# Attention: VectorE's merge of an old unit queued ahead of the newest unit's maximum, and the normalising product of finished rows on GpSimd

## The reference

```
xn = layernorm(x)
q_c = rms_norm(xn @ wq_down.T);  kv_c = rms_norm(xn @ wkv_down.T)
q = [q_c @ wq_up.T | rope(q_c @ wq_rope.T)]          # 16 heads, 128 + 64
k = [kv_c @ wkv_up.T (first 128) | rope(xn @ wk_rope.T)];  v = the other 128
s = softmax(causal(q k^T / sqrt(192))) v, all heads, @ wo.T
g = silu(((silu((xn @ gate_w.T) * gate_s) * ((xn @ up_w.T) * up_s)) @ down_w.T) * down_s)
out = x + s * g
```

## Time and profile before

| | |
|---|---|
| median of the runs shown | 4944.75 us (3 runs: 4944.75, 4978.76, 4425.7) |
| the profiled execution's own time | 4418.68 us |
| span of its slowest core (core 4) | 4417.1 us |
| spans of the eight cores | 4358.2 to 4417.1 us |
| TensorE busy, in the span | 3703.2 us (84%) |
| VectorE busy | 1585.0 us (36%) |
| ScalarE busy | 1189.8 us (27%) |
| GpSimd busy | 382.1 us (9%) |

### The profile page before, as it was taken

The page is one execution under the profiler, slowest core; times in us unless marked ns, Lnnn a source line. Parts: engine busy times, 40 slices in busy tenths (PEclk is TensorE's granted clock), DMA queues, the critical chain, the costliest instruction groups (busy, mean ns, idle before and its releaser), DMA issues.

```text
span 4417.1 us, 57223 instructions; the slowest of 8 cores (4358.2 to 4417.1 us)
## 1 busy us (share of the span) xinstructions
PE 3703.2 (84%) x21727; PEld 1878.3 (43%) x22128; DVE 1585.0 (36%) x3298; ACT 1189.8 (27%) x1591; POOL 382.1 (9%) x487
## 2 busy tenths in 40 slices
PE   1777877777777777777769999999799999999898
PEld 0333334444444444444434444444344444444343
DVE  2445334777677777667821111100001111110000
ACT  1222205555565555555610000000000000000000
POOL 0212230000000000000001111100010000000001
PEclk9888889999999999999989999999899999999999
DMA  8554254676666666676688887865664444435564
GB/s 180 143 141 126 79 138 77 111 114 116 118 114 112 110 108 114 113 116 111 115 153 127 126 128 121 136 204 181 205 194 129 77 77 77 77 68 175 183 194 143
DMA packets 783194, 566.59 MB, mean 128 GB/s; under 512 B 689744, under 2 KB 698192, under 8 KB 773072
## 3 DMA queue, kind: packets, MB, share of 16 engines
q1 hardware_dynamic: 711840, 318.04, 33.5%
q0 software_dynamic: 42288, 171.46, 22.2%
q10 hardware_dynamic: 28800, 73.41, 5.3%
HBM read 499.34 MB, written 73.40 MB: 130 GB/s over the span
## 4 chain that ended last, share of the span: by engine, by line
PE 67%; DVE 16%; DMA 12%; issue 3%; ACT 1%; SPq 0%; POOL 0%; ACTq 0%; DVEq 0%; POOLq 0%
PE bk L1076 25%; PE bk L1096 12%; DVE nmx L897 9%; PE bk L1115 5%; PE ps_s L833 4%; PE ps_o L885 3%; PE ps_mm L427 3%; DMA dw<-d 3%; PE ps_s L838 2%; PE ps_s L867 2%; PE ps_s L845 2%; PE ps_s L864 2%; DMA uw<-upP 2%; DMA pt<-pp 2%; PE ps_kv L427 2%
## 5 line engine op out<-in xcount | busy, mean ns | idle before, releaser
L897 DVE TENSOR_REDUCE nmx<-ps_s 128x1 f32<-128x1024 f32 (+3 forms) x640 | 678.4, 1060 | 416.3 <-PE ps_s L867 254.1
L940 ACT ACTIVATE pp<-ps_s,bia,scq 128x1024 bf16<-128x1024 f32 (+3 forms) x640 | 686.2, 1074 | 525.3 <-DVE bia L901 266.9
L1076 PE MATMUL bk<-xc,gw 128*128 128x512 bf16 x2759 | 639.7, 382 | 53.5 <-DMA uw<-upP 50.6
L1096 PE MATMUL bk<-dw,hdn 128*128 128x512 bf16 x2760 | 615.1, 381 | 52.3 <-DMA dw<-d 48.1
L885 PE MATMUL ps_o<-vv,pt 128*128 128x129 bf16 x4352 | 361.3, 222 | 333.5 <-DVE ost L928 180.6
L1076 PE MATMUL bk<-xc,uw 128*128 128x512 bf16 x2759 | 632.4, 379 | 3.0
L1132 DVE SCALAR_TENSOR_TENSOR hdn<-bk,us_s,sg 128x512 bf16<-128x512 f32 x176 | 131.8, 750 | 1141.7 <-PE bk L1076 1061.9
L885 PEld LDWEIGHTS ps_o<-vv,pt 128*128 128x128 bf16 x4352 | 275.7, 98 | 505.9 <-issue 478.9
L1076 PEld LDWEIGHTS bk<-xc,gw 128*128 128x128 bf16 x2816 | 276.7, 98 | 390.0 <-issue 64.1
L1096 PEld LDWEIGHTS bk<-dw,hdn 128*128 128x128 bf16 x2816 | 275.3, 98 | 390.1 <-issue 66.0
L1164 ACT ACTIVATE sg<-bk,gs_s 128x512 f32<-128x512 f32 x176 | 120.7, 687 | 1110.9 <-PE bk L1076 1067.2
(11 more groups left out here) (101 smaller groups left out, 2663.6 us busy)
## 6 DMA issues: line engine op xcount, KB each, us to landing
dw<-d SPq DMA_DIRECT2D x176, 512.0 KB, 4.8
gw<-gateP POOLq DMA_DIRECT2D x88, 512.0 KB, 6.2
uw<-upP POOLq DMA_DIRECT2D x88, 512.0 KB, 8.4
xb<-xk ACTq DMA_DIRECT2D x32, 1024.0 KB, 6.3
wo_s<-wo SPq DMA_DIRECT2D x16, 2048.0 KB, 9.1
d<-downP POOLq DMA_DIRECT2D x44, 512.0 KB, 12.3
xo<-xk ACTq DMA_DIRECT2D x64, 256.0 KB, 4.4
out<-xo ACTq DMA_DIRECT2D x64, 256.0 KB, 5.7
```

The source lines that it names most:

```text
L897: kb.go(e, lambda: e.tensor_reduce(nmx[n % 8][:], r3(buf(ev_)[:], 2)[:, :, 0:w], AX.XY, ALU.max, negate=True), [("p", f"b_s_{n}")], "v")
L940: kb.go(e, lambda: e.activation(r3(pp[n % NP][:, 0:2 * w], 2), r3(buf(ev_)[:], 2)[:, :, 0:w], AF.Exp, bias=bia[n % 8][:], scale=scq[:, i:i ...
L1076: mm_ = e.matmul(bk[pr * 2 + z][:], W[u_i % 2][:, dc * 128:(dc + 1) * 128], xc[hf][:, dc * 512:(dc + 1) * 512], start=(dc == 0), stop=(dc ...
L1096: mm_ = e.matmul(bk[tt][:], hdn[:, ic * 1024 + hf * 512 + tt * 128: ic * 1024 + hf * 512 + (tt + 1) * 128], dw[q % 3][:, (ic % 4) * 512:(i ...
```

## The change

Four things are done.

1. In `steps()` the merge event of a round is put first: merge(n - 7), S(n), PV(n - 6), piece. On VectorE the merge of unit n - 7 now stands ahead of the maximum of unit n. TensorE's and ScalarE's own orders stay as they are.
2. The normalising product goes from VectorE to GpSimd, a row of the new loop in `b_gp` for each block, and reads oacc and linv from SBUF. So blocks of one unit also are copied to oacc first, and their reciprocal reads oacc. oacc and linv get four buffers; the first merge of a block waits for the product of the block four rows before.
3. The semaphore mark b_mg of a unit is now on its merge in every case; before, that of a block's last unit was on the product.
4. GpSimd's loads and stores stand between the products: the load of wup behind the second product of a head, qp behind the third, the store of the head before behind the seventh. SyncE's transpose of ost is issued one round later and waits for GpSimd's last product.

```diff
-            oacc = [sb(f"oacc{i}", [128, VS], F32) for i in range(3)]
+            oacc = [sb(f"oacc{i}", [128, VS], F32) for i in range(4)]
...
-            linv = [sb(f"linv{i}", [128, 1], F32) for i in range(2)]
+            linv = [sb(f"linv{i}", [128, 1], F32) for i in range(4)]
...
                 for n in range(NU + LAG + 1):
+                    if n >= LAG + 1:
+                        ev.append(("merge", n - LAG - 1))
                     if n < NU:
                         ev.append(("S", n))
                     if n >= LAG and n - LAG < NU:
                         ev.append(("PV", n - LAG))
-                    if n >= LAG + 1:
-                        ev.append(("merge", n - LAG - 1))
...
-                    if ot_next < NH and n >= LASTU[ot_next] + LAG + 3:
+                    if ot_next < NH and n >= LASTU[ot_next] + LAG + 4:
                         h = ot_next
-                        kb.wait(e, "v", f"b_mg_{LASTU[h]}")
+                        kb.wait(e, "g", f"b_on_{h * NB + NB - 1}")
...
                 for h in range(NH):
-                    if h + 2 < NH:
-                        kb.wait(e, "p", f"b_pc_{h}_{NPC - 1}")
-                        load_wup(e, h + 2)
-                    if 1 <= h and h + 1 < NH:
-                        kb.wait(e, "p", f"b_s_{LASTU[h - 1]}")
-                        load_qp(h + 1)
-                    if h >= 1:
-                        store_o(h - 1)
+                    for oi, i in enumerate(BORDER):
+                        row = h * NB + oi
+                        if oi == 0:
+                            kb.wait(e, f"ot{h % 2}", f"b_ot_{h - 2}")
+                        kb.go(e, lambda: e.tensor_scalar(ost[h % 2][:, i * 128:(i + 1) * 128],
+                                                         oacc[row % 4][:, 0:128], linv[row % 4][:], None,
+                                                         ALU.mult, ALU.bypass),
+                              [("g", SELF), ("v", f"b_li_{row}")], "g", f"b_on_{row}")
+                        if oi == 1 and h + 2 < NH:
+                            kb.wait(e, "p", f"b_pc_{h}_{NPC - 1}")
+                            load_wup(e, h + 2)
+                        if oi == 2 and 1 <= h and h + 1 < NH:
+                            kb.wait(e, "p", f"b_s_{LASTU[h - 1]}")
+                            load_qp(h + 1)
+                        if oi == 6 and h >= 1:
+                            store_o(h - 1)
...
-                        if s_ == 0 and ns > 1:
+                        if s_ == 0:
+                            kb.wait(e, "g", f"b_on_{row - 4}")
                             kb.go(e, lambda: e.tensor_copy(A[:, 0:129], O[:, 0:129]),
                                   [("p", f"b_pv_{n}")], "v", f"b_mg_{n}")
-                        elif s_ > 0:
+                        else:
...
                         if s_ == ns - 1:
-                            src = A if ns > 1 else O
-                            L = linv[row % 2]
-                            kb.go(e, lambda: e.reciprocal(L[:], src[:, 128:129]),
-                                  [("p", f"b_pv_{n}"), ("v", SELF)], "v")
-                            kb.go(e, lambda: e.tensor_scalar(dst, src[:, 0:128], L[:], None,
-                                                             ALU.mult, ALU.bypass),
-                                  [("v", SELF)], "v", f"b_mg_{n}")
+                            kb.go(e, lambda: e.reciprocal(linv[row % 4][:], A[:, 128:129]),
+                                  [("v", SELF)], "v", f"b_li_{row}")
```

More of the change, by code:

```diff
@@ L769, in b_sync @@
                 ot_next = 0
-                for n in range(NU + LAG + 4):
+                for n in range(NU + LAG + 5):
                     if n < NU:
@@ L910, in b_vec @@
                         h, i, s_, ns, row = UNITS[n]
-                        A = oacc[row % 3]
+                        A = oacc[row % 4]
                         O = ps_o[n % 2]
-                        dst = ost[h % 2][:, i * 128:(i + 1) * 128]
-                        if n % PER_H == 0:
-                            kb.wait(e, f"ot{h % 2}", f"b_ot_{h - 2}")
-                        if s_ == 0 and ns > 1:
+                        if s_ == 0:
+                            kb.wait(e, "g", f"b_on_{row - 4}")
                             kb.go(e, lambda: e.tensor_copy(A[:, 0:129], O[:, 0:129]),
                                   [("p", f"b_pv_{n}")], "v", f"b_mg_{n}")
-                        elif s_ > 0:
+                        else:
                             kb.go(e, lambda: e.scalar_tensor_tensor(A[:, 0:129], A[:, 0:129], fac[n % 8][:],
```

## The result

The changed kernel is **faster: the ratio to the kernel before is 0.9601, with a 95% interval of 0.956 to 0.9641**. The forecast, 4240 on the level of 4418.7, was a ratio of 0.9596. The profiled execution took 4246.79 us (before 4418.68), 171.9 us less where 177 were forecast. The medians of the runs, 4258.85 us now and 4689.09 us before, hold some executions in which the cores of one die had a lower clock, so the ratio is taken from the others: 4246.3 to 4263.4 us now, 4425.7 and 4433.4 before.

The account below looks back on a forecast made before the run. The loop of maximum, merge and PV between VectorE and TensorE was taken to bound heads with projections. Savings of 153 + 3 + 35 less 14 for DMA make 177 us off 4418.7: 4242, said as 4240, range 4160 to 4335.

Parts of the forecast that it names:

- The bound: In heads 0 to 14 VectorE and TensorE wait for each other in turn, so each projection piece is paid in full.
- part 1: Merge queued ahead of the maximum on VectorE: 10.2 us saved in each of 15 heads, 153 us, and 3 in head 15.
- q pieces: Two projection pieces a head of 24 wide matmuls, 5.2 us each: after the change 3.76 us lost each, 7.5 a head.
- short pieces: Eight projection pieces a head of eight wide matmuls, 1.73 us each: after the change 0.6 us lost each, 4.8 a head.
- the 24.2 us of before: Price of a head's pieces before the change, eight of 1.73 and two of 5.2 us, against 22.5 us seen.
- the ring of score buffers: Three buffers, so scores of round n need the exponential of n-3: the next edge, leaving a lead of 1.44 us.
- Part 2: Normalising product off VectorE: 3.2 us off, 1.0 on for copies, net 2.2 us a head, 35 us in 16 heads.
- Part 3: DMA, the load of wup in its new place among the transposes: 1 us a head added, 14 us, bounds -2 and +5.
- rival (c): The load's stall grows by 5 us a head in its new place: 4296 us, 4310 with the clock's price; chance 0.11.
- (a): GpSimd's product locks VectorE's bias out through a shared port: 26 us at most for the product's bounds; chance 0.05.
- (b): The lead doesn't open because another edge binds where the merge did; only the product's gain stays: 4384 us; chance 0.12.
- (d): Short pieces vanish wholly and q pieces mostly, so a head comes near TensorE's own time, 77 us: 4147 us; chance 0.10.

Follow-up runs that it names:

- the three products: The changed kernel with each normalising product on GpSimd issued three times, holding the same values: no ratio, two shortest executions 4254.26 and 4227.25 us.
- the best version: The changed kernel with the load of wup behind the sixth product, the ring's mark ahead of fac and q pieces halved: ratio 0.9423, 4139.8 to 4150.5 us.

## Why the prediction came out as it did

**The bound and part 1: right.** The heads were bound by the loop of maximum, merge and PV. The order alone took 9.8 us off an undisturbed head against 10.2, and 2.9 off head 15 against 3. The terms hold as well: in head 14 of that kernel VectorE idles 3.9 and 4.1 us behind the two q pieces, 8.0 where 7.5 were worked out, and 5.2 us otherwise, where 4.8 were put for the short pieces. (One price was off there: I put all eight short pieces at 1.73 us, but the four of v take 1.95 by the earlier trace rows, which makes the 24.2 us of before 25.1.) The long waits that are left stand behind q pieces, as the model had it (in the changed kernel a q piece at 1435.6 in head 8 is followed by a maximum after 4.43 us of idling; 3.76 were worked out). The next edge is the ring of score buffers, as said. What I left out there is that the ring's mark is on fac, 0.28 us behind the exponential, where I took 0.1 us for the whole hand-over. The run with the mark moved prices that at 1.25 us a head. Take it off the 13.3 us of idling in the run with the order alone and 12.0 are left, against 12.3 in the model. That subtraction is an estimate, for the mark wasn't moved in that kernel.

**Part 2: mis-sized.** The step that failed is "from one to the next maximum 0.20, so 3.2 us off", with "a copy and the wait of the reciprocal for it 1.0 us on". VectorE's work went down by 5, not 2.2. Where nothing idles, in head 15, merge to maximum at a block's end was 0.39 + 0.20 + 0.20 = 0.79 us before and is 0.39 + 0.08 = 0.47 after. The maximum needs nothing of the reciprocal and follows it closely, so taking out one instruction also freed its neighbour: 0.32 in each of 12 blocks. For the four blocks of one unit bias to maximum was 0.78 (bias to reciprocal 0.31, then 0.20 and 0.27) and is 0.59 with the copy in the kernel with the product alone, where the same kind of bias stands ahead: 0.19 less, not more. The copy starts 0.19 us behind the start of a bias it doesn't depend on. (In the changed kernel it is 0.53, but 0.06 of that is the shorter bias that the new order puts ahead.) Such a block in head 15, before and with the product alone:

```profile
2195.41 0.28 DVE L905 TENSOR_SCALAR bia<-nmx,scq,bia 128x1 f32<-128x1 f32 x1
2195.72 0.17 DVE L926 RECIPROCAL linv<-ps_o 128x1 f32<-128x1 f32 x1
2195.92 0.35 DVE L928 TENSOR_SCALAR ost<-ps_o,linv 128x128 bf16<-128x128 f32 x1
2196.19 1.21 DVE L897 TENSOR_REDUCE nmx<-ps_s 128x1 f32<-128x1024 f32 x1
```

```profile
2109.36 0.27 DVE L913 TENSOR_SCALAR bia<-nmx,scq,bia 128x1 f32<-128x1 f32 x1
2109.55 0.28 DVE L923 COPY oacc<-ps_o 128x129 f32<-128x129 f32 x1
2109.87 0.16 DVE L930 RECIPROCAL linv<-oacc 128x1 f32<-128x1 f32 x1
2109.95 1.22 DVE L905 TENSOR_REDUCE nmx<-ps_s 128x1 f32<-128x1024 f32 x1
```

Together 12 x 0.32 + 4 x 0.19 = 4.6 us, against 4.7 and 4.9 in the run with the product alone.

But part 2 also said that VectorE was "full or paying for each gap", so that each of its microseconds counts. With the new order it didn't hold: 5 us less work gave 2.8 us less head, since the ring's edge stood beside it and the rest came back as idle time (13.3 to 15.2). In head 15, with no pieces, all of it counts, and with it the last 1.4 us of idle time: 72.4 to 66.1 us. That the two errors nearly cancel in an undisturbed head, 82.4 forecast and 82.2 found, is luck.

**Part 3: mis-sized, and rival (c) was half true.** I put the load's new place at 1 us a head with bounds of -2 and +5. What stands above an undisturbed head went from 3.0 us (97.85 - 94.8) to 5.5 (87.75 - 82.2) on the slowest cores, and from 1.7 to 4.2 in the mean of the eight: 2.5 more either way, inside the bounds. The step that failed is the use of the 12.11 us landing for the new place: I named the transpose of ost as a neighbour there and then gave it no price, and behind it a landing took 17.68. Head 12 of all cores has such a stall and alone makes 14.5 of the 54.4 us; in the other heads the stalls are shorter, and why they too are longer than before is argued, not shown: SyncE's issue of the transpose of ost (median 1.9 us) stands ahead of the next transpose of pp, and the load is under way beside both. This also tells where the gain of the product went. It is worth 2.8 us a head on top of the order, and the load's place, which came with it, costs 2.5 more. Hence the order alone, at 0.966, can't be told from the whole change at 0.9601: their intervals overlap. With the load moved, the product's share shows (0.9494, in which the 1.3 us a head of stalls that the order alone keeps is gone as well).

**Rivals.** (a) fell with the three products; a product takes 0.601 us, and 0.5 was taken. (b) fell: heads are 82, not 92. (c) came with half its size. (d) didn't come: the ring keeps 15 us of idling, and even the best version stays 2 us above the 77 of that rival.

**Total.** Forecast 177 us, found 163.7 in attention: head 15 gained 4.0 more (it has no piece for the ring to hold up), head 0 2.0 less, heads 1 to 13 17 less, mostly the stalls (13 x 1.5 = 20). That the profile shows 171.9 owes 7.7 us to an earlier start that isn't of the change's making.

## What to carry to other kernels

Where two engines each look partly idle, find the loop in which they wait for each other, and ask of each queue whether work on an old tile stands behind a wait for the newest; moving it ahead costs nothing while the wait is long enough to cover it. Price an instruction that leaves a queue by the distance between its neighbours afterwards, not by its own, and then check which edge is next, as the rest of the saving comes back as idle time (here 2.8 of 5 us came through). DMA issues that move along with an edit are a part of it: look at which transposes a large load will meet, and try it in more than one place. And read the stalls on all cores, as the slowest core is the one with the most of them.

## What was unexpected of the hardware

- A load of 640 KB issued by GpSimd close behind a transpose of 128 x 2048 sometimes held both up. On one core at a distance of 0.7 us they took 16.2 and 19.7 us to landing, with a transpose of pp at 17.68 us where 3.2 is the median; on all eight cores in head 12, at 0.37 to 0.39 us, the load took 14.3 to 20.3. In the other loads at 0.7 us it took 8.6 in the median. Four rows of queries (about 20 us) later the same load, 7.0 us to landing, made no engine wait. In the stretch of 1126 to 1157 us shown above the load's queue moved 0.92 MB in 240 packets, 3.8 KB each, and the transposes' 2.10 MB in 8491 packets, 0.25 KB each. The Trainium skill, "DMA: Bandwidth & Descriptors", section "Queues, rings and completion order", says that a DMA engine takes turns between its queues packet by packet and drains a packet whole. With packets 15 times as large on one side a transpose would fall behind, so the trace agrees in direction, if the profile's packets are those of the page. It doesn't tell the good place of the load from the bad, for around a load there (core 2, 1148 to 1160 us) the packets are 4.6 and 0.25 KB; no run here changed the size of a packet.
- After a stall TensorE comes back slow. In the 11 us without a matmul and the 9 us behind them (clock in the third column from the end), the granted clock was 0.56 and then 0.79 of full speed in the mean, so at the lower of the levels of 1.2 and 2.4 GHz for most of the first stretch and for a part of the second; in the 16 us from 1164 on it was 1.00:

```profile
1143.90:1155.00 11.10, 0.00 (x0) 0.00 (x0) 0.40 (x2) 0.00 (x0) 0.00 (x0) 0.56 1.24 103
1155.00:1164.00 9.00, 8.77 (x92) 6.75 (x93) 4.64 (x10) 5.48 (x9) 0.00 (x0) 0.79 0.91 158
```

- Head 15 kept pace at a DMA share of 0.90 with no idle time of VectorE ahead of its maxima, so a high share of the DMA engines alone doesn't stall the transposes.
